# Features in 32x64 tiles from compact transposed probabilities, and a saturating addition for q's clip

## The chip, the cores and the metric

The kernel runs on one core of a Trainium2 chip. The metric is device time in microseconds, as the median of several runs. Five engines work side by side, each through its own program: TensorE (PE; its weight loads are listed as PEld), VectorE (DVE), ScalarE (ACT), GpSimd (POOL) and SyncE (SP), which only starts transfers here. They wait for each other by semaphores. The kernel is written in Bass: each engine's order is the order in which its program is written out, and no scheduler moves anything.

## The reference

```python
def attn(x, Wq, bq, Wk, bk, Wv, bv, Wo, bo):      # after the GRU, x is [128 (b), 32 (t), 256]
    q, k, v = x @ Wq + bq, x @ Wk + bk, x @ Wv + bv
    ...                                            # reshape to 4 heads of 64, over 32 positions
    weights = softmax(einsum('bdsh,bdth->bdst', q, k) / sqrt(d))
    feats = einsum('bdst,bdth->bdsh', weights, v)
    return feats.reshape(B, S, F) @ Wo + bo
def derivative(q, p, drive, coupling, bias):
    dq = q - q ** 3 / 3.0 - p + drive + tanh(q) @ coupling.T + bias
    dp = EPSILON * (q + ALPHA - BETA * p)
    return dq, dp
def rk4_step(q, p, drive, coupling, bias):
    ...                                            # four derivatives, at 0, DT/2, DT/2, DT
    q_next = clip(q + DT / 6.0 * (dq1 + 2 * dq2 + 2 * dq3 + dq4), -CLAMP, CLAMP)
    p_next = clip(p + DT / 6.0 * (dp1 + 2 * dp2 + 2 * dp3 + dp4), -CLAMP, CLAMP)
    return q_next, p_next
def ffn(x, w_gate, w_up, w_down):                  # bitlinear: 8-bit rows, ternary weights
    return bitlinear(silu(bitlinear(x, w_gate)) * bitlinear(x, w_up), w_down)
x = x + attn(gru(cond_2048, x, ...), ...)
x = x + ffn(rk4(cond_2048, cond_2048, x, ...), ...)
```

## The kernel before

The kernel works in three stages.

**The GRU**, 32 steps, up to 209 us. TensorE holds it; q and k of the attention are made beside it. Nothing of it is changed.

**Attention**, 209 to 294.5 us, in 8 rounds of 16 batch rows (4 groups `g` of 128 columns, each with 4 rows of 32 positions, `quads` j). In round i TensorE runs scores(i) (L374, 64 calls on tiles of 64 rows and 32 columns), values(i, 0) (L396, 12 matmuls), in three rounds a weight sum (L416), project(i-2, 0) (L436, 6 matmuls of 512 columns), values(i, 1), project(i-2, 1) and feats_of(i-1) (L410, 16 calls). An fp32 call of scores or feats appears as two matmuls and two weight loads. VectorE runs the softmax of the round (L934 maximum, L938 subtraction, L942 sum, L944 reciprocal, L946 product into `Pn`), then `turn(i)` (L955): four transposes of 32x512, one for each quad, put the 32x32 blocks of P on the diagonal of a 128x128 block of `PT`, whose other places are zero (GpSimd's two memsets L1243 at the stage's start, `s_zero`). So feats_of multiplies four batch rows at once with K = 128, three quarters of it zeros. Then `keep_feats` (L961) makes the low half of the features that `project` reads, once ScalarE has made the high half (L693), and `residual` (L967) adds the projection to x. ScalarE copies scores and values out of PSUM (L685, L678) and takes the exponential (L726).

**The RK4 and FFN stage**, 294.5 to 601.7 us, 32 steps t of four slots each. A slot starts with a seed that VectorE writes into PSUM (seed_1 L1042, seed_2 L1046, seed_3, seed_4), ScalarE makes tanh in two halves m (L756) and the scaled square (L759), TensorE adds the coupling and identity products to the seed (L461), VectorE makes w = cubic (L1066) and with L1072 the next point from PSUM and w. The last slot's L1072 writes to another part of PSUM (columns 128 to 256), and the clip L1161 makes q of the next step from it. GpSimd keeps the chain of p: v1 (L1273), uz (L1276), u3 (L1277), t1 (L1282), W3 (L1290), WZ (L1299), dq, and p of the next step (L1304); VectorE continues t1 to t2 (L1110), t3 and t4 (L1154). In the same step the FFN of earlier steps runs in a pipeline: `product` (L1085) multiplies the up projection (L560, four matmuls of 416 columns) with silu(gate), in two halves; the first half of step t-2 stands on VectorE right behind seed_1 of step t. ScalarE turns the product to integers (L775), TensorE transposes them (L497), ScalarE copies (L781).

Semaphores that matter: `s_next` counts L1072 (8 per step), `s_q` the clips (2 per step), `s_seed` the seeds (8 per step), `s_up` the up projections.

## Time and profile before

| | us |
|---|---|
| median of 3 runs | 604.24 (603.88 to 604.67) |
| the profiled execution, its own time | 603.75 |
| its span, first to last instruction | 601.7 |
| GRU, attention, last stage | 209.0, 85.5, 307.2 |
| busy: TensorE, VectorE, ScalarE, GpSimd | 572.9, 513.5, 390.1, 254.0 |
| mean granted TensorE clock | 0.997 |

Everything below is read from the one profiled execution. "issue" as the end of an idle time means that the engine waited for nothing that the profile shows. Busy times of matmuls are modelled, and neighbouring ones overlap a little.

### The profile page before, as it was taken

The page shows a single profiled execution, that of the slowest core. Times are in us where ns is not written, and L with a number is a line of the kernel's source. Part 1 is how long each engine was busy: PE and PEld are TensorE (multiplying, and loading weights), DVE is VectorE, ACT ScalarE, POOL GpSimd, SP SyncE. Part 2 cuts the span into 40 slices and gives each one's busy share as a digit, 9 for nine tenths or more (in the row PEclk, how much of TensorE's full clock was granted, in tenths as well). Part 3 has the DMA queues.
Part 4 walks back from the last instruction along what each step waited for, and adds up shares of the span by engine and source line. Part 5 has one row for each costly group of instructions (what it writes and reads, how often), then busy time and mean ns, then how long its engine had stood idle before and what let it go on. Part 6 is the DMA issues. An engine that isn't in the chain of part 4 may idle for free.

```text
span 601.7 us, 15742 instructions
## 1 busy us (share of the span) xinstructions
PE 572.9 (95%) x5692; PEld 521.0 (87%) x5692; DVE 513.5 (85%) x1547; ACT 390.1 (65%) x959; POOL 254.0 (42%) x401
## 2 busy tenths in 40 slices
PE   9999999999999988999978999999999999999997
PEld 8999999999999887888867788888888888888885
DVE  3777767776777768998999999999999999999996
ACT  3554454444544453464556888898898888888885
POOL 0423323233232264240155556556555555555550
PEclk9999999999999998999999999999999999999999
DMA  8500000000000000500000000000000000000001
GB/s 259 187 2 2 1 1 2 1 1 2 1 1 1 19 3 2 190 4 3 1 1 1 11 19 16 15 19 10 18 20 10 19 20 10 19 19 11 17 19 37
DMA packets 12523, 14.97 MB, mean 25 GB/s; under 512 B 1632, under 2 KB 10144, under 8 KB 12448
## 3 DMA queue, kind: packets, MB, share of 16 engines
q1 hardware_dynamic: 12448, 13.97, 7.0%
q8 instruction: 47, 0.77, 0.5%
q14 instruction: 28, 0.23, 0.1%
HBM read 9.78 MB, written 4.19 MB: 23 GB/s over the span
## 4 chain that ended last, share of the span: by engine, by line
PE 73%; DVE 13%; ACT 11%; issue 3%; DVEq 0%; POOL 0%; ACTq 0%; POOLq 0%
PE PS L461 23%; PE PS L313 17%; PE PS L336 13%; ACT q_s L775 5%; PE PS L436 4%; PE PS L513 4%; PE PS L534 3%; PE PS L497 3%; ACT k_s L756 2%; DVE big L955 2%; PE PS L396 2%; PE PS L319 2%; DVE PS L1072 1%; ACT PS L759 1%; DVE h_s L1161 1%
## 5 line engine op out<-in xcount | busy, mean ns | idle before, releaser
L461 PE MATMUL PS<-k_s,h_s 128*128 128x128 f32 x1024 | 160.6, 284 | 4.2 <-DVE PS L1046 2.0
L461 PEld LDWEIGHTS PS<-k_s,h_s 128*128 128x128 f32 x1024 | 131.7, 191 | 21.1 <-DVE PS L1060 9.8
L313 PE MATMUL PS<-part 128*128 128x256 f32 x900 | 115.6, 286 | 0.0
L313 PEld LDWEIGHTS PS<-part 128*128 128x128 f32 x900 | 109.8, 191 | 0.0
L756 ACT ACTIVATE k_s<-h_s 128x128 f32<-128x128 f32 x256 | 69.1, 306 | 49.8 <-DVE h_s L1161 29.0
L336 PE MATMUL PS<-big,wrk 128*128 128x128 f32 x744 | 88.4, 275 | 1.7 <-DVE big L913 1.7
L336 PEld LDWEIGHTS PS<-big,wrk 128*128 128x128 f32 x744 | 85.8, 192 | 2.3 <-DVE big L913 2.3
L1229 POOL COPY h_s<-big 128x256 f32<-128x256 f32 x32 | 21.5, 671 | 128.9 <-DVE big L913 128.9
L461 PE MATMUL PS<-h_s 128*128 128x128 f32 x384 | 74.3, 275 | 0.0
L461 PEld LDWEIGHTS PS<-h_s 128*128 128x128 f32 x384 | 58.3, 192 | 0.0
L650 ACT ACTIVATE big<-big 128x256 f32<-128x256 f32 x32 | 13.3, 416 | 63.2 <-DVE big L895 63.2
L1066 DVE SCALAR_TENSOR_TENSOR h_s<-PS,h_s 128x256 f32<-128x256 f32 x128 | 52.7, 412 | 0.3 <-ACT PS L759 0.2
L1072 DVE SCALAR_TENSOR_TENSOR h_s<-PS,h_s 128x128 f32<-128x128 f32 x192 | 50.1, 285 | 2.2 <-PE PS L461 0.8
L759 ACT ACTIVATE PS<-h_s 128x256 f32<-128x256 f32 x128 | 47.2, 369 | 1.4 <-DVE part L961 1.4
L640 ACT ACTIVATE big<-PS,bg 128x256 f32<-128x256 f32 x96 | 41.2, 467 | 6.8 <-DVE bg L852 5.8
L1085 DVE SCALAR_TENSOR_TENSOR q_s<-PS,q_s 128x416 f32<-128x416 f32 x64 | 41.0, 644 | 0.8 <-PE PS L560 0.8
L652 ACT ACTIVATE big<-big 128x256 f32<-128x256 f32 x32 | 13.4, 418 | 38.9 <-DVE big L903 38.9
L1304 POOL TENSOR_SCALAR h_s<-q_s 128x256 f32<-128x256 f32 x31 | 12.5, 402 | 59.0 <-DVE q_s L1154 59.0
L1290 POOL TENSOR_TENSOR h_s<-h_s,k_s 128x256 f32<-128x256 f32 x32 | 25.0, 780 | 29.1 <-DVE q_s L1110 27.9
L899 DVE SCALAR_TENSOR_TENSOR big<-PS,bh,big 128x128 f32<-128x128 f32 x64 | 19.5, 346 | 18.0 <-ACT big L650 18.0
L1299 POOL TENSOR_TENSOR q_s<-h_s,k_s 128x256 f32<-128x256 f32 x32 | 23.9, 748 | 23.2 <-DVE PS L1052 23.2
L775 ACT ACTIVATE q_s<-q_s,mag 128x832 f32<-128x832 f32 x29 | 30.9, 1067 | 0.0
(189 smaller groups left out, 1244.9 us busy)
## 6 DMA issues: line engine op xcount, KB each, us to landing
out<-q_s SPq DMA_DIRECT2D x32, 128.0 KB, 1.7
x_s<-in_xT SPq DMA_DIRECT2D x14, 256.0 KB, 6.1
k_s<-in_wgT SPq DMA_DIRECT2D x1, 832.0 KB, 5.3
k_s<-in_wuT SPq DMA_DIRECT2D x1, 832.0 KB, 7.2
k_s<-in_wih SPq DMA_DIRECT2D x3, 256.0 KB, 4.1
wrk<-in_whh SPq DMA_DIRECT2D x3, 256.0 KB, 4.3
h_s<-in_wdT SPq DMA_DIRECT2D x1, 768.0 KB, 7.5
x_s<-in_xT SPq DMA_DIRECT2D x4, 128.0 KB, 3.6
```

The source lines that it names most:

```text
L313: r = pe.matmul(p, y, x, start=i == 0, stop=i == len(passes) - 1)
L336: r = pe.matmul(PS[:, bank, m * 128:(m + 1) * 128], whh_s[:, k, (m0 + m) * 128:(m0 + m + 1) * 128], hprev[:, k, :], start=k == 0, stop=k == 1)
L436: r = pe.matmul(PS[:, bank, :], raw(w), raw(x), start=k == 0 and n == 0, stop=k == 1 and n == 2)
L461: return pe.matmul(PS[:, m, 0:128], w, x, start=False, stop=True, skip_group_check=True)
L640: ac.activation(gi[:, n % 2, m, :], bulk_bank(u), ACT.Identity, bias=bg[:, m:m + 1]).then_inc(s_gi, 1)
L756: ac.activation(cm(th[slot % 2], m), cm(src, m), ACT.Tanh).then_inc(s_th, 1)
L759: ac.activation(sqP, src, ACT.Square, scale=math.sqrt(cube[s])).then_inc(s_sq, 1)
L775: ac.activation(hf[:, 0:NI], hN[i % 2], ACT.Identity, scale=h_at(i, 4), bias=mag[:, 0:1]).then_inc(s_hf, 1)
L1066: ve.scalar_tensor_tensor(w_, sqP, cube[s] * own[s], src, ALU.subtract, ALU.mult).then_inc(s_w, 1)
L1072: ve.scalar_tensor_tensor(dst(m), PS[:, m, 0:128], of_ps[slot % 4], cm(w_, m), ALU.mult, ALU.subtract).then_inc(s_next, 1)
L1085: ve.scalar_tensor_tensor(hN[i % 2][:, at], pg[:, g], q_at(i, 3), sg[:, at], ALU.mult, ALU.mult).then_inc(s_hN, 1)
L1290: po_.tensor_tensor(two(W3), two(u3), I_at(t), ALU.add).then_inc(s_W3, 1)
```

## The change

Attention. The probabilities stay compact: `PT` is 128x512, and `turn` is one 128x512 transpose (the engine's transpose works in 32x32 blocks). feats_of makes 64 calls of K = 32, M = 64, N = 32 in 32x64 tiles in place of 16 of K = 128, M = 64, N = 128. The features stand in PSUM by quads (banks 4 to 7; in round 7 banks 1 and 2, in two halves with a wait between them), project reads them by a strided view, and the other banks move with them: values 4 to 2, project and the keep-warm matmuls 7 to 3. The memsets and `s_zero` go, values(0, 0) no longer waits for `s_qka`, and VectorE's keep_feats waits for both of ScalarE's halves.

Last stage. q and p are kept multiplied by lam = 3/c4, so that the last slot's new q is PS + w without a factor. A custom VectorE operation (`TENSOR_ADD_SAT`, addition with two limits) writes q in place of L1072 and L1161; the seeds, tanh and squares take the factor back in their scale. seed_1 waits for `s_q` and becomes a scalar_tensor_tensor. On GpSimd v1 stands behind the wait for seed_1, and t1 ahead of uz and u3.

```diff
-        PT = [big[:, 2048 + 2048 * r:4096 + 2048 * r].rearrange("p (u n) -> p u n", u=16) for r in range(2)]
+        PT = [big[:, 2048 + 512 * r:2560 + 512 * r] for r in range(2)]
...
-        feats = [PS[:, 5:7, :]] * 7 + [PS[:, 3:5, :]]
+        fb = lambda a, n: PS[:, a:a + n, :].rearrange("p b (h n) -> p (b h) n", h=2)
+        feats = [PS[:, 4:8, 0:256]] * 7 + [fb(1, 2)]
+        of_g = lambda a: a.rearrange("p (j g t) -> p g j t", j=4, g=4)
...
                 if (i, hf) == (0, 0):
                     pe.wait_ge(s_wv, 2)
                     pe.wait_ge(s_vs0, 1)
-                    pe.wait_ge(s_qka, 1)
...
                 pe.wait_ge(s_PT, i + 1)
-                for g in range(4):
-                    for hd in range(4):
-                        a = 64 * (hd % 2)
-                        r = pe.matmul(feats[i][a:a + 64, hd // 2, g * 128:(g + 1) * 128], Vs[i % 2][:, g, hd * 64:(hd + 1) * 64],
-                                      PT[i % 2][:, unit(g, hd), :], start=True, stop=True)
+                for js in ((0, 2), (1, 3)) if i == 7 else ((0, 1, 2, 3),):
+                    if js == (1, 3):
+                        r.then_inc(s_pv7, 1)
+                        pe.wait_ge(s_pv7, 1)
+                    for g in range(4):
+                        for kk in range(2):
+                            for j in js:
+                                for a in (0, 64):
+                                    hd = 2 * kk + a // 64
+                                    r = pe.matmul(feats[i][a:a + 64, j, (4 * kk + g) * T:(4 * kk + g + 1) * T],
+                                                  Vs[i % 2][quads[j], g, hd * 64:(hd + 1) * 64],
+                                                  PT[i % 2][quads[j], unit(g, hd) * T:(unit(g, hd) + 1) * T],
+                                                  start=True, stop=True)
                 r.then_inc(s_pv, 1)
...
             def turn(i):
-                if i < 2:
-                    ve.wait_ge(s_zero, i + 1)
-                else:
+                if i >= 2:
                     ve.wait_ge(s_pv, i - 1)
                 ve.wait_ge(s_P, i + 1)
-                for r in quads:
-                    o = ve.transpose(PT[i % 2][r, :, r], Pn[r, :, :])
-                o.then_inc(s_PT, 1)
+                ve.transpose(PT[i % 2], Pn.rearrange("p u n -> p (u n)")).then_inc(s_PT, 1)
...
                 for m in range(2):
                     if t:
-                        ve.wait_ge(s_next, 8 * t - 1 + m)
-                    ve.tensor_tensor(PS[:, m, 0:128], I_at(t)[:, m], cm(pn[t % 2], m), ALU.subtract).then_inc(s_seed, 1)
+                        ve.wait_ge(s_q, 2 * t - 1 + m)
+                    ve.scalar_tensor_tensor(PS[:, m, 0:128], cm(pn[t % 2], m), -1 / lam, I_at(t)[:, m], ALU.mult,
+                                            ALU.add).then_inc(s_seed, 1)
...
+            def last_next(t):
+                ve.wait_ge(s_w, 4 * t + 4)
+                for m in range(2):
+                    ve.wait_ge(s_ps, 8 * t + 7 + m)
+                    ve._custom_dve(bass.dve_ops.TENSOR_ADD_SAT, out=cm(qn[(t + 1) % 2], m), in0=PS[:, m, 0:128],
+                                   in1=cm(w_, m), s0=CLAMP * lam, s1=-CLAMP * lam).then_inc(s_q, 1)
...
-                nexts(4 * t + 3, lambda m: PS[:, m, 128:256])
-                for m in range(2):
-                    ve.wait_ge(s_next, 8 * t + 7 + m)
-                    ve.tensor_scalar(cm(qn[(t + 1) % 2], m), PS[:, m, 128:256], CLAMP, -CLAMP, ALU.min,
-                                     ALU.max).then_inc(s_q, 1)
+                last_next(t)
...
                     po_.wait_ge(s_q0, 1)
+                if t:
+                    po_.wait_ge(s_seed, 8 * t + 2)
                 if t < T - 1:
                     po_.tensor_scalar(v1, p, horner[0], 0.0, ALU.mult, ALU.add).then_inc(s_v1, 1)
-                if t:
-                    po_.wait_ge(s_seed, 8 * t + 2)
-                po_.tensor_scalar(uz, p, -n3, 0.0, ALU.mult, ALU.add).then_inc(s_uz, 1)
-                po_.tensor_scalar(u3, p, -n2, 0.0, ALU.mult, ALU.add).then_inc(s_u3, 1)
-                if t < T - 1:
-                    if t:
-                        po_.wait_ge(s_q, 2 * t)
                     po_.wait_ge(s_v1, t + 1)
                     po_.tensor_tensor(t1, v1, q, ALU.add).then_inc(s_t1, 1)
+                po_.tensor_scalar(uz, p, -n3 / lam, 0.0, ALU.mult, ALU.add).then_inc(s_uz, 1)
+                po_.tensor_scalar(u3, p, -n2 / lam, 0.0, ALU.mult, ALU.add).then_inc(s_u3, 1)
```

TensorE's order from values ahead of feats(0) to scores(3), before (`big` holds values and PT, `part` the split halves, `k_s,q_s` keys and queries):

```order
L396 MATMUL PS<-part 128x256 x24
L410 MATMUL PS<-big 64x128 x16
L374 MATMUL PS<-k_s,q_s 32x32 x64
L396 MATMUL PS<-part 128x256 x12
L436 MATMUL PS<-part 128x512 x6
L396 MATMUL PS<-part 128x256 x12
L436 MATMUL PS<-part 128x512 x6
L410 MATMUL PS<-big 64x128 x16
L374 MATMUL PS<-k_s,q_s 32x32 x64
```

and after:

```order
L400 MATMUL PS<-part 128x256 x24
L420 MATMUL PS<-big 64x32 x64
L379 MATMUL PS<-k_s,q_s 32x32 x64
L400 MATMUL PS<-part 128x256 x12
L448 MATMUL PS<-part 128x512 x6
L400 MATMUL PS<-part 128x256 x12
L448 MATMUL PS<-part 128x512 x6
L420 MATMUL PS<-big 64x32 x64
L379 MATMUL PS<-k_s,q_s 32x32 x64
```

The same places in the same order; L410's 16 calls have become L420's 64, directly ahead of the 64 of scores.

VectorE at the end of a step and the start of the next, before (`h_s` and `q_s` hold the step's buffers, `k_s` the drive and tanh):

```order
L1154 SCALAR_TENSOR_TENSOR q_s<-q_s,h_s 128x256
L1157 RECIPROCAL q_s<-q_s 128x1
L1072 SCALAR_TENSOR_TENSOR PS<-PS,h_s 128x128 x2
L1161 TENSOR_SCALAR h_s<-PS 128x128 x2
L1042 TENSOR_TENSOR PS<-k_s,h_s 128x128 x2
L1085 SCALAR_TENSOR_TENSOR q_s<-PS,q_s 128x416
L1066 SCALAR_TENSOR_TENSOR h_s<-PS,h_s 128x256
L1102 TENSOR_REDUCE q_s<-PS 128x1
```

and after:

```order
L1174 SCALAR_TENSOR_TENSOR q_s<-q_s,h_s 128x256
L1177 RECIPROCAL q_s<-q_s 128x1
L1092 ISA h_s<-PS,h_s 128x128 x2
L1054 SCALAR_TENSOR_TENSOR PS<-h_s,k_s 128x128 x2
L1105 SCALAR_TENSOR_TENSOR q_s<-PS,q_s 128x416
L1079 SCALAR_TENSOR_TENSOR h_s<-PS,h_s 128x256
L1122 TENSOR_REDUCE q_s<-PS 128x1
```

The two clips are gone, and the last slot's two L1072 are the two L1092; nothing else has moved.

GpSimd over the same turn, from p of the next step (L1304, after: L1315), before:

```order
L1304 TENSOR_SCALAR h_s<-q_s 128x256
L1273 TENSOR_SCALAR h_s<-h_s 128x256
L1276 TENSOR_SCALAR h_s<-h_s 128x256
L1277 TENSOR_SCALAR h_s<-h_s 128x256
L1282 TENSOR_TENSOR q_s<-h_s 128x256
L1290 TENSOR_TENSOR h_s<-h_s,k_s 128x256
```

and after:

```order
L1315 TENSOR_SCALAR h_s<-q_s 128x256
L1289 TENSOR_SCALAR h_s<-h_s 128x256
L1291 TENSOR_TENSOR q_s<-h_s 128x256
L1292 TENSOR_SCALAR h_s<-h_s 128x256
L1293 TENSOR_SCALAR h_s<-h_s 128x256
L1301 TENSOR_TENSOR h_s<-h_s,k_s 128x256
```

t1, the tensor_tensor into `q_s`, stands two places earlier.

## Rows read from the trace of the kernel before

**Rows 1.** Busy time by stage: stretch, length, PE, PEld, DVE, ACT, POOL, clock, DMA share.

```profile
209.00:294.50 85.50, 79.16 (x1600) 69.57 (x1600) 74.19 (x126) 43.98 (x68) 31.07 (x25) 0.98 0.11 36
294.50:601.70 307.20, 287.56 (x2365) 246.65 (x2363) 293.26 (x1067) 248.81 (x634) 160.68 (x278) 1.00 0.05 15
```

**Rows 2.** The page: the chain that ended last, by line.

```profile
PE PS L461 23%; PE PS L313 17%; PE PS L336 13%; ACT q_s L775 5%; PE PS L436 4%; PE PS L513 4%; PE PS L534 3%; PE PS L497 3%; ACT k_s L756 2%; DVE big L955 2%; PE PS L396 2%; PE PS L319 2%; DVE PS L1072 1%; ACT PS L759 1%; DVE h_s L1161 1%
```

**Rows 3.** TensorE's timeline, attention: start, us, engine, line, operation, [idle before it].

```profile
212.45 1.66 PE L396 MATMUL PS<-part 128*128 128x256 f32 x12 [0.21 <-ACT q_s L671]
...
217.68 1.03 PE L374 MATMUL PS<-k_s,q_s 64*32 64x32 f32 x97 [0.45 <-issue]
...
221.06 1.69 PE L396 MATMUL PS<-part 128*128 128x256 f32 x12 [0.69 <-ACT big L678]
222.91 1.97 PE L410 MATMUL PS<-big 128*64 128x128 f32 x32 [0.17 <-DVE big L955]
...
226.37 0.34 PE L374 MATMUL PS<-k_s,q_s 64*32 64x32 f32 x26 [0.48 <-issue]
226.64 1.70 PE L396 MATMUL PS<-part 128*128 128x256 f32 x12
230.63 2.78 PE L436 MATMUL PS<-part 128*128 128x512 f32 x6 [2.29 <-DVE part L961]
...
238.44 1.29 PE L374 MATMUL PS<-k_s,q_s 64*32 64x32 f32 x128
...
241.19 1.55 PE L436 MATMUL PS<-part 128*128 128x512 f32 x6
...
247.39 1.40 PE L374 MATMUL PS<-k_s,q_s 64*32 64x32 f32 x128
```

**Rows 4.** Stretches around project(0,0), TensorE alone; PEclk is the third number from the end.

```profile
230.50:232.00 1.50, 1.37 (x4) 0.59 0.00 0
232.00:234.00 2.00, 2.00 (x8) 0.50 0.03 8
```

**Rows 5.** VectorE's timeline, the first two turns.

```profile
219.92 2.85 DVE L955 STREAM_TRANSPOSE big<-big 32x512 f32<-32x512 f32 x4
...
226.85 2.85 DVE L955 STREAM_TRANSPOSE big<-big 32x512 f32<-32x512 f32 x4
```

**Rows 6.** The page, DMA queues: packets, MB, share of 16 engines.

```profile
q8 instruction: 47, 0.77, 0.5%
```

**Rows 7.** DMA traffic between 223.2 and 226.4, in 40 slices of 0.08 us.

```profile
DMA  0000000000700000000000000000000000000000
...
q8 instruction: 1, 0.02, 1.9%
```

**Rows 8.** TensorE's timeline, the last scores and values.

```profile
275.82 1.29 PE L374 MATMUL PS<-k_s,q_s 64*32 64x32 f32 x128
277.04 0.50 PE L396 MATMUL PS<-part 128*128 128x256 f32 x2
277.74 1.36 PE L396 MATMUL PS<-part 128*128 128x256 f32 x10 [0.20 <-issue]
```

**Rows 9.** All engines' timeline, the turn of one step into the next of the last stage.

```profile
488.11 0.87 PE L560 MATMUL PS<-h_s,q_s 128*128 128x416 bf16 x4
...
488.30 0.48 DVE L1161 TENSOR_SCALAR h_s<-PS 128x128 f32<-128x128 f32 x2
...
488.70 0.49 DVE L1042 TENSOR_TENSOR PS<-k_s,h_s 128x128 f32<-128x128 f32 x2
488.70 0.27 PEld L486 LDWEIGHTS PS<-ident,h_s 128*128 128x128 f32 x2
...
489.10 0.65 DVE L1085 SCALAR_TENSOR_TENSOR q_s<-PS,q_s 128x416 f32<-128x416 f32 x1
...
490.55 0.55 PE L497 MATMUL PS<-identh,q_s 128*128 128x128 f16 x7 [0.35 <-ACT q_s L775]
...
491.42 0.79 POOL L1290 TENSOR_TENSOR h_s<-h_s,k_s 128x256 f32<-128x256 f32 x1 [0.68 <-DVE q_s L1110]
```

**Rows 10.** VectorE's timeline, the first product of the last stage.

```profile
316.70 0.65 DVE L1085 SCALAR_TENSOR_TENSOR q_s<-PS,q_s 128x416 f32<-128x416 f32 x1 [0.80 <-PE PS L560]
```

More of the change, by code:

```diff
@@ L200, in build @@
         s_bulk, s_gi, s_qk, s_qka = sem("s_bulk"), sem("s_gi"), sem("s_qk"), sem("s_qka")
[L202 to L203 removed]
+        s_wv, s_vs0, s_wo, s_vhi, s_split = (
+            sem(n) for n in ("s_wv", "s_vs0", "s_wo", "s_vhi", "s_split"))
+        s_pv7 = sem("s_pv7")
         s_S, s_Vp, s_pv, s_o = sem("s_S"), sem("s_Vp"), sem("s_pv"), sem("s_o")
@@ L395, in values @@
                             pe.wait_ge(s_vs0, 2)
-                        r = pe.matmul(PS[:, 4, (g % 2) * 256:(g % 2) * 256 + 256], raw(x), raw(w), start=n == 0,
+                        r = pe.matmul(PS[:, 2, (g % 2) * 256:(g % 2) * 256 + 256], raw(x), raw(w), start=n == 0,
                                       stop=n == 5)
@@ L415, in weight_sum @@
                 pe.wait_ge(s_abs, w + 1)
-                pe.matmul(PS[:, 7, w:w + 1], ones[:, :], wsum[:, w:w + 1], start=True, stop=True).then_inc(s_wsum, 1)
+                pe.matmul(PS[:, 3, w:w + 1], ones[:, :], wsum[:, w:w + 1], start=True, stop=True).then_inc(s_wsum, 1)
             def project(i, m):
@@ L1241, in gpsimd @@
             po_.wait_ge(s_hb, T)
-            for r in range(2):
-                po_.memset(PT[r][:, :, :], 0.0).then_inc(s_zero, 1)
             for i in range(9):
```

80 lines of the change are left out of this document (42 added, 38 removed).

## The prediction

> **What bounds the kernel now.** The stages were read first. The GRU (0 to 209 us) is not touched by the change. Attention takes 85.5 us and TensorE is busy for 79.2 of them; the RK4/FFN stage takes 307.2 us, with VectorE busy for 293.3 and TensorE for 287.6 [rows 1]. The chain of work that ended last names L461 first, and counts the clip L1161 at only 1% [rows 2], so the last stage is a hand-over between TensorE, VectorE and ScalarE and not one engine's load.
>
> In attention I read TensorE's timeline, then what released it. From 238.44 to 247.39, scores(3) to scores(4), one round takes 8.95 us and nothing in it waits: TensorE is the bound there. The one long wait is 2.29 us ahead of the first project at 230.63, for VectorE's keep_feats [rows 3]. VectorE gets there late because each turn of P is four transposes, 2.85 us [rows 5]. After that idle stretch the granted clock is 0.59 and then 0.50 of full [rows 4], that is 1.2 GHz instead of 2.4, and the six matmuls of that project take 2.78 us where the same six take 1.55 later [rows 3].
>
> The same timeline shows something smaller that I take to decide this case. Twice a row of scores is cut by a gap put down to "issue": 0.45 us ahead of 217.68, with 97 of the 128 matmuls still to come, and 0.48 us ahead of 226.37, with 26 to come [rows 3]; a third gap, 0.20 us, stands at 277.74 [rows 8]. Each matmul has one weight load beside it (2365 and 2363 in the last stage, [rows 1]), so between the first two gaps lie 2 x (97 + 12 + 12 + 32 + 102) = 510 instructions, two times 255: the rest of scores(1), two halves of values, feats(0) and the head of scores(2). The page counts 47 instruction packets of 0.77 MB in all [rows 6], 16 KB each. One of them starts in the tenth of the 40 slices between 223.2 and 226.4, at 224.0; it takes 1.9% of 16 engines' 3.2 us, 0.97 us [rows 7], and TensorE goes on at 226.37. So TensorE's program seems to come in blocks of some 256, and a block cannot begin before its packet, asked for when the block before it began, has arrived. The lower bound from block start to block start: 2 x 102 = 204 instructions of scores(2) and 52 of the 64 of feats(0) ahead of the gap put the last start near 222.91 + 12 x 0.03 = 223.3, and it resumed at 226.37, so **3.1 us**. For the third gap, 252 instructions ahead of the two values matmuls, the start is that of scores(7), 275.82, and the resumption 277.74: **1.9 us** [rows 8].
>
> **The change, part by part.** Sums are against the profiled execution, 603.75 us; the median of before is 604.24, so 0.5 is added at the end.
>
> (a) Turn. One 128x512 transpose in place of four 32x512 ones. Four cost 2.85 us, one of 32x512 about 0.70; the elements per partition are the same, so I take 0.70 (lower end: 0.69 as an elementwise operation; upper end 2.85, if the 128 rows were worked off in fours). Saved 2.15 per block on VectorE. Two such turns precede keep_feats(0) [rows 5], 4.3 us, more than the wait of 2.29 [rows 3]: the wait goes, and next late is TensorE itself. With it the half clock goes: 2.78 - 1.55 = 1.2 us on the project and some 0.4 on the values behind it, together **-3.9**. In the later blocks TensorE does not wait for VectorE, and the saving there is worth nothing on the path.
>
> (b) Feats. 16 calls (32 matmuls, 1.97 us [rows 3]) become 64 calls, 128 matmuls and 128 weight loads, of a quarter of the columns. Each works in its own 32x64 tile, eight fit the array at once. The nearest row is scores, also 128 matmuls on eight tiles: 1.29 us. The other end is today's 1.97 or somewhat over, should the 64-column loads set the pace. I take 1.29, -0.68 for each of the six feats that stand in TensorE-bound rounds, **-4.1**.
>
> (c) Start. values(0,0) no longer waits for s_qka; project and feats banks change places; the GpSimd memsets go. 0.21 of wait at 212.45 and 0.17 ahead of feats(0) [rows 3]: **-0.4**. Today's issue gaps, 0.93 in all, are partly absorbed by the wait for L678 that follows: counted in (d).
>
> (d) Instruction blocks. In today's rounds feats (64) and scores (256) make 320 fast instructions. After, feats(i-1) and scores(i+1) stand back to back (TensorE's order in the section on the change), 512 fast ones in 2.6 us. Wherever the boundary falls, one whole block of 256 lies inside such a row, and takes 1.3 us where at least 1.9 to 3.1 are needed. That is a stall of 0.6 to 1.8 us in each of six rounds, and nothing covers it, since TensorE is the bound. The block behind the first row is short also, up to 1.0. Between 1.9 and 3.1 I take 2.9, since two of three gaps show 3.1: 6 x 1.6 + 1.0 = 10.6 us, against some 0.6 of today's gaps that this replaces: **+10.0**.
>
> The Trainium skill (Runtime: NRT & Kernel Launch, Instruction fetch mechanics) says that programs are refilled in blocks of 256 instructions and that crossing a boundary is "mostly hidden"; the block size agrees with the distance of the gaps here, the hiding not: 0.45 and 0.48 us are open. By its rule (d) would be near nothing, which is rival 1.
>
> (e) The clip. Two clips (0.48 the pair, 0.40 from the first to the seeds behind them) and the step through PSUM go; a saturating addition in place of L1072 writes q. The chain view suggests 0.2 from the clip and 0.2 from tanh, earlier by as much: 0.4 a step. But it buys only the time until the next thing that VectorE waits for: the product L1085 at 489.10, behind four L560 matmuls that begin at 488.11 and end at 488.98, and no later than these allow [rows 9]. In step 2 the same product visibly waits 0.80 for L560 [rows 10]. L560 stands on TensorE behind its own queue, which the clip doesn't move. From L1085 on VectorE runs without a gap to the next seed, and TensorE's pass L497 waits for ScalarE at the same time, 490.55. So the clip's 0.4 becomes wait ahead of L1085. I take 0.01 a step, 0.3 in all (0 to 0.08 x 31), and 0.4 for the first step, where no product stands: **-0.7**.
>
> (f) The saturating addition itself is not in the trace. Nearest: a two-input operation on 128x128 from PSUM or to it, 0.49 the pair (L1042), 0.20 apart. A custom one may be as fast, or slower by some tenths; up to 0.3 more a step disappears in the wait that (e) opens; beyond it each 0.1 costs 3 us. I take 0. Seeds change form at the same 0.29. Scales in tanh and square ride in the same instruction: 0.
>
> (g) GpSimd. v1 waits for the seeds now and t1 comes ahead of uz and u3. Same instructions, same wait ahead of W3 for VectorE's t2 (0.68 idle, [rows 9]); the held 0.41 fits into it: 0.
>
> **Sum.** -3.9 -4.1 -0.4 +10.0 -0.7 = +0.9: 604.65 for the profiled execution, 605.1 on the median. By the ends of block time alone: 1.9 gives 6 x 0.6 = 3.6 in (d), 598; 3.1 gives 606.3; if feats keep today's 1.97 with 3.1, (b) is nothing, a block in the row takes 1.3 to 2.0 and each stall is some 0.35 shorter, 608.3. As two of three gaps stand at the upper end, and (b) can only be worse than taken, I put the forecast a little above the sum, **605.6 us**.
>
> **Rivals.** 1. Blocks arrive ahead (faster). Then (d) is -0.6 to +3.6 and the kernel lands at 595 to 599. For it: the third gap's 1.9, and the last stage runs without such gaps; against it, 256 of its instructions take 16.6 us (4728 in 307.2, [rows 1]). By the skill's rule (above) this is the case. 0.25. 2. The hand-over pays (faster). The chain view is right, L560 comes early too, and each step is 0.3 to 0.4 shorter: -9 to -12 on top, 595. Against: L1085 starts right at the end of L560. 0.09. 3. The idle stretches of (d) bring back the half clock (slower). 2.29 us of idle did it once [rows 3, 4] and cost 1.6; stalls of 1.6 to 1.8 in each round could, 0.45 did not. From 1.6 us idle on it decides: three to six times 1.6 on 605, or feats at 1.97 and more: 609 to 613. 0.15. 4. The addition does not do what it is for (no change of its own, or slower by 0.1 to 0.2 beyond its cover): +3 to +6, 608 to 611. 0.06. The forecast's own case (602.5 to 608): 0.45.
>
> **How the numbers follow.** 0.2% (1.2 us) is about what a measurement of this kernel can tell from none: 603.0 to 605.4 is no change. The main case puts 0.04 under it, 0.17 within, 0.24 over. With rivals 1 and 2 faster has 0.37, with 3 and 4 slower 0.45, the rest 0.18. For 8 in 10 the range reaches from 596.5, inside rivals 1 and 2, to 611, inside rival 3.
>
> **What would show it.** In the changed profile: (a) L955 once per block at 0.7, no wait ahead of project(0,0), clock 1.0 to 294 us. (b) L420, 128 matmuls, 1.3 us when not cut. (d) in six rounds an "issue" idle of 1 to 2 us inside L420 or L379, at distances of 256 instructions. If these gaps are under 0.5, rival 1 holds; if the clock falls behind them, rival 3. (e) L1105 with an idle of 0.3 to 0.4 for TensorE's L560 successor in each step, and the last stage within 1 us of its 307.2; one shorter by 9 or more is rival 2. (f) L1092 at 0.28 to 0.30. The forecast is wrong most likely in the block time, which rests on three gaps.

## The result, and the profile after

The changed kernel takes **621.84 us** (median of 4 runs, 620.37 to 626.09), the kernel before 604.06 beside it. The ratio is 1.031, with a 95% interval of 1.029 to 1.034. It is slower, as forecast, but by 18 us where the forecast said 1.5, and outside the range of 596.5 to 611. The profiled execution took 621.29 us with a span of 619.3, 17.6 us more than before.

The page of the changed kernel: the instruction packets, and the chain that ended last by engine.

```profile
q8 instruction: 53, 0.87, 0.6%
...
PE 79%; DVE 12%; issue 6%; ACT 2%; DVEq 0%; POOL 0%; POOLq 0%
```

53 packets in place of 47 [rows 6], and "issue", time in which an engine waited for nothing that the profile shows, is now 6% of the chain (3% before). Busy time by stage (columns as in [rows 1]), over fixed stretches:

```profile
209.00:294.50 85.50, 69.65 (x2069) 61.99 (x2067) 48.93 (x78) 37.82 (x58) 24.83 (x15) 0.88 0.11 36
294.50:619.00 324.50, 300.79 (x2668) 259.06 (x2668) 296.62 (x1029) 258.68 (x645) 164.77 (x286) 0.99 0.04 15
```

Between 209 and 294.5 us, where TensorE was busy for 79.2 us [rows 1], it is busy for 69.7 now at a mean clock of 0.88, and attention isn't over. Its last projects start at 304.14 and the keep-warm matmuls behind them at 311.29; before, the keep-warm matmuls started at 294.39. So 16.9 us of the 17.6 are there by the start of the last stage. Of these 0.7 lie ahead of attention: every step of the GRU comes 0.73 later from the first on, since the opening matmuls are slower in this execution (the first 24 of L318 take 5.90 us for 5.35). TensorE's timeline in attention (start, us, engine, line, operation, idle before it) answers to [rows 3]:

```profile
223.34 1.49 PE L420 MATMUL PS<-big 32*64 32x32 f32 x128
...
225.90 1.24 PE L379 MATMUL PS<-k_s,q_s 64*32 64x32 f32 x122 [0.88 <-issue]
...
229.46 0.99 PE L400 MATMUL PS<-part 128*128 128x256 f32 x7 [1.53 <-issue]
230.28 1.57 PE L448 MATMUL PS<-part 128*128 128x512 f32 x6
...
238.97 0.45 PE L379 MATMUL PS<-k_s,q_s 64*32 64x32 f32 x32 [1.90 <-issue]
...
253.32 1.00 PE L379 MATMUL PS<-k_s,q_s 64*32 64x32 f32 x70 [4.59 <-issue]
254.25 2.93 PE L400 MATMUL PS<-part 128*128 128x256 f32 x12
256.98 2.73 PE L448 MATMUL PS<-part 128*128 128x512 f32 x6
...
277.50 0.43 PE L379 MATMUL PS<-k_s,q_s 64*32 64x32 f32 x21 [2.00 <-issue]
...
302.15 2.06 PE L420 MATMUL PS<-big 32*64 32x32 f32 x102 [1.34 <-issue]
304.14 7.32 PE L448 MATMUL PS<-part 128*128 128x512 f32 x24
```

The long wait for L961 ahead of the first project (230.63 in [rows 3]) is gone, and feats takes 1.49 instead of 1.97. But ten gaps with the releaser "issue" add up to 15.4 us: 0.46, 0.88, 1.53, 1.90, 4.59, 0.45, 0.51, 2.00, 1.73 and 1.34. Matmuls and weight loads counted together in the trace, with the few records of TensorE's sequencer between them, each of these gaps stands 256 or 512 instructions behind the one before, to within one. And what follows five of the six gaps over 1.3 us (not the 1.53) is slow: twelve values matmuls take 2.93 us where 1.69 is usual, six project matmuls 2.73 where 1.57 is, the last 24 7.32. The windows show the clock there (stretch, length, PE busy, PEclk, DMA share, GB/s):

```profile
249.00:253.30 4.30, 0.00 (x0) 0.93 1.04 397
253.30:259.50 6.20, 6.18 (x88) 0.50 0.18 56
...
304.00:311.30 7.30, 7.30 (x36) 0.77 0.01 2
```

Behind the gap of 4.59 us TensorE runs at 0.50 of the full clock, the level of 1.2 GHz, for 6 us, and the last projects have 0.77 on the mean. And in that gap the transfers run at 397 GB/s: the FFN's weights.

The last stage, the turn of a step, answers to [rows 9]; behind it the one line of who held up L1105:

```profile
505.45 0.29 DVE L1092 CUSTOM_DVE_ANT_0 h_s<-PS,h_s 128x128 f32<-128x128 f32 x1 [0.17 <-PE PS L473]
505.47 0.87 PE L572 MATMUL PS<-h_s,q_s 128*128 128x416 bf16 x4
505.66 0.49 DVE L1054 SCALAR_TENSOR_TENSOR PS<-h_s,k_s 128x128 f32<-128x128 f32 x2
...
506.31 0.41 POOL L1289 TENSOR_SCALAR h_s<-h_s 128x256 f32<-128x256 f32 x1 [0.80 <-DVE PS L1054]
...
506.45 0.65 DVE L1105 SCALAR_TENSOR_TENSOR q_s<-PS,q_s 128x416 f32<-128x416 f32 x1 [0.30 <-PE PS L572]
...
507.86 0.41 POOL L1293 TENSOR_SCALAR h_s<-h_s 128x256 f32<-128x256 f32 x1
...
508.08 0.34 DVE L1059 SCALAR_TENSOR_TENSOR PS<-h_s,k_s 128x128 f32<-128x128 f32 x1
```

```profile
  PE PS L572: 9.9, 30
```

The addition L1092 takes 0.29, seed_1 follows at once, and VectorE then idles for 0.30 until the up projection is done: 9.9 us in 30 steps. Steps are 9.12 us apart in place of 9.08.

### The profile page after: what moved, and what is told of

Its sections match the earlier page's. It is cut to its first block, busy times and chain, and to the rows that moved or that the text cites. A ratio compares the mean times of both kernels' runs of the same rounds, so it can differ in the third digit from the quotient of the medians.

```text
span 619.3 us, 17184 instructions
## 1 busy us (share of the span) xinstructions
PE 576.7 (93%) x6460; PEld 526.0 (85%) x6460; DVE 490.8 (79%) x1459; ACT 393.5 (64%) x959; POOL 251.5 (41%) x399
## 4 chain that ended last, share of the span: by engine, by line
PE 79%; DVE 12%; issue 6%; ACT 2%; DVEq 0%; POOL 0%; POOLq 0%
PE PS L473 23%; PE PS L318 17%; PE PS L341 12%; PE PS L400 5%; PE PS L448 4%; PE PS L572 4%; PE PS L525 4%; PE PS L546 3%; DVE q_s L1105 3%; DVE h_s L1085 2%; DVE q_s L1122 2%; PE PS L420 2%; PE PS L379 2%; PE PS L324 2%; DVE PS L1059 1%
## 5 line engine op out<-in xcount | busy, mean ns | idle before, releaser
L318 PE MATMUL PS<-part 128*128 128x256 f32 x900 | 115.6, 286 | 0.0
L318 PEld LDWEIGHTS PS<-part 128*128 128x128 f32 x900 | 109.8, 191 | 0.0
L769 ACT ACTIVATE k_s<-h_s 128x128 f32<-128x128 f32 x256 | 72.3, 307 | 47.2 <-DVE h_s L1085 29.4
L1085 DVE SCALAR_TENSOR_TENSOR h_s<-PS,h_s 128x128 f32<-128x128 f32 x192 | 50.1, 285 | 2.1 <-PE PS L473 0.8
L1105 DVE SCALAR_TENSOR_TENSOR q_s<-PS,q_s 128x416 f32<-128x416 f32 x64 | 41.0, 643 | 9.9 <-PE PS L572 9.9
L1315 POOL TENSOR_SCALAR h_s<-q_s 128x256 f32<-128x256 f32 x31 | 12.5, 402 | 59.0 <-DVE q_s L1174 59.0
L400 PE MATMUL PS<-part 128*128 128x256 f32 x192 | 31.5, 320 | 2.3 <-issue 1.5
```

The lines of the kernel that those rows point to most:

```text
L318: r = pe.matmul(p, y, x, start=i == 0, stop=i == len(passes) - 1)
L400: r = pe.matmul(PS[:, 2, (g % 2) * 256:(g % 2) * 256 + 256], raw(x), raw(w), start=n == 0, stop=n == 5)
L769: ac.activation(cm(th[slot % 2], m), cm(src, m), ACT.Tanh, scale=(-1 if s == 3 else 1) / lam).then_inc(s_th, 1)
L1085: ve.scalar_tensor_tensor(dst(m), PS[:, m, 0:128], of_ps[slot % 4], cm(w_, m), ALU.mult, ALU.add if slot % 4 == 2 else ALU.subtract).then_ ...
L1105: ve.scalar_tensor_tensor(hN[i % 2][:, at], pg[:, g], q_at(i, 3), sg[:, at], ALU.mult, ALU.mult).then_inc(s_hN, 1)
```

## The experiments

Theory: TensorE's program arrives in blocks of 256 instructions, at a limited rate; feats and scores back to back use them up faster, and the clock falls by half behind the idle time. In the last stage, the clips' time has turned into a wait for the up projection. Runs in which one part is done alone, undone or mended follow, and a direct measurement.

### Each half of the change alone

att_only is the attention part on the last stage of before, last_only the other way round.

> The attention part of the change on the last stage of before. Theory (program blocks arrive late where feats and scores stand back to back, and the idle time halves the clock): the whole loss is here. The attention stage is longer than the kernel before's by 15 to 17 us, 'issue' gaps of 0.5 to 4.6 us inside L420/L379, and the last stage keeps its 9.08 us period: 619 to 622 us. Rival (the loss is half in the last stage, from the custom addition and the moved GpSimd order): 611 or less.

> The last-stage part alone (scaling, saturating addition, GpSimd order), attention as in before. Theory: the clip's time becomes a wait for the up projection (L572 in the changed kernel), and the period goes from 9.08 to 9.13 us as in the changed kernel: 604.5 to 605.5 us. Rival (the last stage gains once attention no longer disturbs it): a period of 8.7 to 9.0 us, 592 to 602 us.

Measured: att_only 622.98 us (618.37 to 624.96, ratio 1.031, 1.026 to 1.036); last_only 604.16 (603.52 to 605.78), ratio 1.0014, 0.9998 to 1.003. The whole loss is in attention. The steps of att_only's last stage are the 9.08 us of before, those of last_only 9.12. On the whole time the last-stage part is worth nothing, either way.

### Is it the number of instructions?

padded is the kernel before, with small calls on constants behind feats(0) to feats(5):

```diff
                 r.then_inc(s_pv, 1)
+                if i < 6:
+                    for n in range(48):
+                        j, c = n // 2 % 2, 64 * (n % 2)
+                        at = 32 * (n // 4)
+                        pe.matmul(PS[c:c + 64, 2 + j, at:at + 32], ones[32 * j:32 * j + 32, 0:64],
+                                  ones[32 * j:32 * j + 32, 0:32], start=True, stop=True)
```

> The kernel before, whole, with 48 extra small matmul calls (96 matmuls and 96 weight loads on constants, into unused banks) right behind each of feats(0) to feats(5), so that 256 instructions of feats and padding stand ahead of the 256 of scores as in the changed kernel; turn, banks and last stage are those of before. Theory (the number of instructions back to back makes the gaps): 'issue' gaps of 1 to 2 us in most of the six rounds, one of 3 to 5 near 250 us where the weights are loaded, half clock behind those over 1.5: 3 to 5 us for the padding itself and 12 to 20 for the gaps, 618 to 628 us. Rival (the strided reads, the 32-row tiles or the new banks of the changed feats make them): 607 to 610 us, gaps as in before.

Measured: 625.22 us (623.64 to 626.03), ratio 1.036, 1.033 to 1.038. The gaps come at the same instructions as in the changed kernel (ahead of the last 32, 70, 21 and 61 matmuls of a row of scores), each by 0.3 to 0.5 us shorter. TensorE's timeline of padded:

```profile
241.60 0.36 PE L374 MATMUL PS<-k_s,q_s 64*32 64x32 f32 x32 [1.62 <-issue]
...
257.55 1.00 PE L374 MATMUL PS<-k_s,q_s 64*32 64x32 f32 x70 [4.16 <-issue]
...
283.60 0.33 PE L374 MATMUL PS<-k_s,q_s 64*32 64x32 f32 x21 [1.49 <-issue]
...
297.20 0.79 PE L374 MATMUL PS<-k_s,q_s 64*32 64x32 f32 x61 [1.34 <-issue]
```

The transpose, the strided reads and the banks of the changed feats are not in this kernel, so they do not make the gaps. What it shares with the changed kernel is the number of instructions, and also the 32x64 tiles of the padding calls; that such tiles stand without gaps when slow instructions lie between them is shown by feats_mixed below. The padding took 1.6 us a round, twice what I had expected. Up to the keep-warm matmuls padded is 21.8 us behind the kernel before: some 9 us are the padding's own work, 9.9 the gaps (11.0 less 1.1 of before), and half clock adds some 5 us more than before, against the wait of 2.29 us, which is gone.

### Fast instructions apart

feats_apart issues feats_of(i-1) between values(i,0) and project(i-2,0), feats_mixed between project(i-2,0) and values(i,1). The edit of feats_mixed:

```diff
-                if i == 8:
-                    feats_of(7)
...
                     project(i - 2, 0)
+                if 1 <= i < 9:
+                    feats_of(i - 1)
                 if i < 8:
                     values(i, 1)
...
-                if 1 <= i < 8:
-                    feats_of(i - 1)
```

> The changed kernel with feats_of(i-1) issued between values(i,0) and project(i-2,0), so that 24 values and 12 project instructions stand between each 256 of scores and each 256 of feats; the same instructions and the same work. Theory: every block of 256 now holds at least 36 slow instructions and lasts some 4 us, longer than the 3.1 to 3.3 us from block to block: no 'issue' gap over 0.5 us from the third round on, clock 1.0, attention 8 to 9 us shorter than in before, 596 to 598 us. Rival 1 (small tiles themselves slow the supply of instructions, wherever they stand): gaps stay, 615 to 620. Rival 2 (gaps come whenever a block is under 5 us, since packets queue behind the weight loads): one gap of 2 to 4 us at 250 us stays, 600.

Measured: 613.38 us (612.0 to 613.78), ratio 1.016, 1.013 to 1.018. That is 8.5 less than the changed kernel, not the 24 that I expected. Its timeline:

```profile
233.92 0.31 PE L420 MATMUL PS<-big 32*64 32x32 f32 x7 [1.76 <-issue]
...
242.84 0.69 PE L420 MATMUL PS<-big 32*64 32x32 f32 x45 [0.27 <-issue]
...
254.52 1.06 PE L420 MATMUL PS<-big 32*64 32x32 f32 x83 [3.01 <-issue]
...
294.51 8.66 PE L448 MATMUL PS<-part 128*128 128x512 f32 x24 [0.69 <-DVE x_s L977]
```

My sum was wrong for the side with values only. A block that spans scores, the 24 instructions of values and feats takes 1.69 + 1.1 to 1.2, not 4 us, and so three gaps of 0.2 to 0.3 stay in the later rounds, one of 1.76 ahead of 233.92 and 3.01 at the weight loads. The gap of 1.76 was not followed by half clock: from 231 to 240 us the clock was 1.00. The end is also slow: 24 projects in 8.66 us, at a mean clock of 0.65.

> The changed kernel, with feats_of(i-1) between project(i-2,0) and values(i,1): 36 slow instructions on either side of each 256 fast ones from the third round on, the same instructions in all. Theory: a block of 256 takes at least 3.2 + 1.1 = 4.3 us, more than 3.3, so no 'issue' gap from scores(3) on but the one near 250 us (2 to 3 us, behind the weight loads); the first three rounds keep theirs: 605 to 609 us. Rival (the supply is slower than 4.3 us per 256 once it has to catch up): gaps in every round, over 612.

Measured: 611.11 us (610.09 to 613.08), ratio 1.012, 1.009 to 1.015, above the 605 to 609 that I expected. Its timeline:

```profile
236.62 1.29 PE L379 MATMUL PS<-k_s,q_s 64*32 64x32 f32 x128
...
245.31 1.29 PE L379 MATMUL PS<-k_s,q_s 64*32 64x32 f32 x128
...
251.81 1.11 PE L420 MATMUL PS<-big 32*64 32x32 f32 x90 [1.60 <-issue]
...
289.90 2.58 PE L448 MATMUL PS<-part 128*128 128x512 f32 x6 [3.46 <-DVE x_s L977]
292.41 3.95 PE L420 MATMUL PS<-big 32*64 32x32 f32 x128
296.29 6.41 PE L448 MATMUL PS<-part 128*128 128x512 f32 x18
```

From 234 to 286 us the rounds now run without a gap but for 1.60 behind the weights and one of 0.75. (Three waits of 0.25 for the weight sums are there as before.) scores(4) follows scores(3) by 8.69 us where 8.95 stood before [rows 3]: 0.26 us is what the small tiles give a round when the program keeps up, under half of the 0.68 of my term (b). That the time is still 611 lies mostly in the end: project(6,0) waits 3.46 us for residual(5,0), which VectorE does last, feats(7) takes 3.95 at 0.50 of the clock, and the 18 projects behind it 6.41, part of them at half clock (0.66 on the mean).

### The weight loads

loads_apart is the changed kernel with the four loads issued at four places, mixed_loads_pool adds that and GpSimd's old order to feats_mixed:

```diff
-            sp.wait_ge(s_Vp, 8)
-            sp.dma_start(coup, kp(coupT)).then_inc(ld_coup, 16)
             for i, w in enumerate((wgT, wuT)):
+                sp.wait_ge(s_Vp, 8 + i)
                 sp.dma_start(halves(w_src[i]), kp(w)).then_inc(ld_w[i], 16)
+            sp.wait_ge(s_Vp, 11)
```

> The changed kernel, with the 2.8 MB of weights that are issued together after values(3,1) issued one by one: w_gate then, w_up after values(4,0), w_down after values(5,0), coupling after values(6,0). Theory (the packet of the program waits behind these loads): the gap of 4.59 us falls to 1.7 to 2.5, and no new one over 2.5 appears: 2 to 3 us less than the changed kernel, 618 to 620. Rival (that gap has another cause): it stays at 4 to 5 us, 621 to 622.

Measured: 618.88 us (618.16 to 621.32), ratio 1.026, 1.023 to 1.029. The time is in the range of the theory; the gap of 4.59 is 2.71 here, a little over the 2.5 that I had as its bound, and the one ahead of it 2.06:

```profile
240.33 0.47 PE L381 MATMUL PS<-k_s,q_s 64*32 64x32 f32 x32 [2.06 <-issue]
...
252.59 0.81 PE L381 MATMUL PS<-k_s,q_s 64*32 64x32 f32 x70 [2.71 <-issue]
```

> The last two edits together, and GpSimd's old order. Theory: the three effects add up: no gap over 0.5 us from scores(3) on, clock 1.0 there, period of a step 9.08 us: 599 to 603 us. Rival (the load of weights moves into blocks that were not short of time before, or the late weights hold up ScalarE): 604 to 608.

Measured: 610.4 us (609.54 to 612.65), which is feats_mixed again. The rival holds in what it says of the gap; its 604 to 608 left out the slow end, which this kernel shares with feats_mixed. The gap at 251.81 is gone, and a new one stands just behind the third load, w_down, which is issued at 257.69:

```profile
264.61 0.42 PE L422 MATMUL PS<-big 32*64 32x32 f32 x2 [3.51 <-issue]
```

By the count of instructions the block before the gap started at 259.07, right behind that load, and its packet of the program started only at 261.97, 2.9 us later. The loads of w_gate and w_up, issued at 244.46 and 248.72, delayed the next packets too (they started 2.1 and 1.8 us behind their blocks' starts), but those blocks took 4.2 to 4.4 us to work off, and no gap of note came. So not every load of 0.8 MB costs a gap; spacing alone moved this one.

### The end, and loads in a chain

mixed_tail is feats_mixed with feats_of(7) ahead of project(6,0) again, and residual(5,0) earlier on VectorE:

```diff
-                if 2 <= i < 7:
+                if i >= 2:
                     residual(i - 2, 0)
                 if i == 7:
                     weight_top(0, 0)
...
-            residual(5, 0)
             residual(5, 1)
```

> The changed kernel with feats_of(0 to 6) between project and values(i,1) as in the run feats_mixed, feats_of(7) back ahead of project(6,0), and residual(5,0) ahead of normal(7) on VectorE. Theory: the idle 3.46 us ahead of project(6,0) and the half clock behind it (L448 x18 in 6.41 us, L420 in 3.95) fall away, the rest is as in feats_mixed: 602 to 605 us. Rival (project(6,0) waits for keep_feats(6) anyway and the clock halves as in feats_apart): 607 to 610.

Measured: 607.0 us (604.69 to 607.24), ratio 1.006, 1.004 to 1.008; its profiled execution took 604.69. The wait of 3.46 us is gone and the clock is 1.00 in the last 10 us of attention. The median lies at the edge of the rival, the profiled execution in the range of the theory. The first three rounds still carry 4.1 us of gaps (0.80, 0.86, 0.86, 1.53), the weights 1.49. That is what this feats costs with the order mended: it is no gain yet.

mixed_tail_chained_split issues each piece of the weights when the last has landed (w_down follows in the same way in three pieces, and the coupling weights come last instead of first):

```diff
             for i, w in enumerate((wgT, wuT)):
-                sp.dma_start(halves(w_src[i]), kp(w)).then_inc(ld_w[i], 16)
+                for k in range(2):
+                    sp.dma_start(halves(w_src[i])[:, k], kp(w)[:, k]).then_inc(ld_w[i], 16)
+                    sp.wait_ge(ld_w[i], 16 * k + 16)
```

and signals the up projection by halves (next section).

> The run mixed_tail, with the FFN weights loaded in seven pieces of 0.26 to 0.43 MB, each issued when the one before has landed, and the up projection split. Theory: the 1.6 us gap near 250 us and the half clock behind it shrink (a packet of the program waits for one piece, 1 us), -2 to -3 us, and the last stage gives 6 to 9: 592 to 597 us. Rival (the chain of pieces comes too late for ScalarE's weight_abs, or the last stage does not pay): 600 to 604.

Measured: **595.39 us** (594.04 to 598.79), ratio 0.987, 0.985 to 0.990. That is in the range of the theory. Beside 0.59, 0.60, 0.85 and 0.22 in the first rounds its remaining gaps in attention are:

```profile
229.27 0.99 PE L404 MATMUL PS<-part 128*128 128x256 f32 x7 [1.53 <-issue]
...
261.02 0.30 PE L424 MATMUL PS<-big 32*64 32x32 f32 x2 [0.77 <-issue]
```

No gap stands near 250 us any more: there the packets start 1.0 to 1.2 us behind the start of their blocks, where it was 3.7 in the changed kernel. The mean clock of the profiled execution is 1.0. Two edits meet in this run, but they act in different stages. The keep-warm matmuls start at 291.0 us (294.4 in before, 294.6 in mixed_tail), and from there to the end it takes 301.0 us (307.3 and 308.1). So of the gain on before some 3.4 us are attention and 6.2 the last stage. Chained loads were not tried on the kernel before, which had no gap at its loads.

### What the clips were worth

Both kernels get the same edit, the one before and the last-stage part of the change: the up projection is signalled after two of its four matmuls, and the product's first half waits for these alone.

```diff
                     for g in range(2):
                         for k in range(2):
                             r = pe.matmul(pg[:, g], qiT[:, k, :], wu_q[:, k, g * 416:(g + 1) * 416],
                                           start=k == 0, stop=k == 1)
-                    r.then_inc(s_up, 1)
+                        r.then_inc(s_up, 1)
...
-                    ve.wait_ge(s_up, i + 1)
+                    ve.wait_ge(s_up, 2 * i + 1)
                     product(i, 0)
```

> The kernel before, with the up projection L560 signalled after each half, so that the product's first half (L1085) waits for two of its four matmuls, 0.4 us earlier. Theory (in before the product starts when the clips and the seeds ahead of it on VectorE are done, which is the same moment as the end of L560): 0 to 0.1 us per step at most, 601.5 to 604.5 us. Rival (L560 alone sets the product in before): 0.3 to 0.4 per step, 592 to 595 us.

> The last-stage part of the change alone, with the same split of the up projection. Theory (the clips' 0.4 us has become a wait for the up projection, 0.30 us per step in the changed kernel): with the product's first half waiting for half of it the wait goes, and the period falls from 9.13 to 8.8 to 8.9 us: 595 to 598 us. Rival (TensorE or ScalarE sets the period as soon as VectorE has slack): 9.05 or more, 602 to 604.

Measured: before_up_split 602.14 us (601.8 to 603.49), ratio 0.998, 0.997 to 0.999, with steps of 9.07; last_up_split **598.17** (596.64 to 599.05), ratio 0.991, 0.989 to 0.993, with steps of mostly 8.89. VectorE in last_up_split, and below it GpSimd in the same stretch:

```profile
502.53 0.29 DVE L1083 CUSTOM_DVE_ANT_0 h_s<-PS,h_s 128x128 f32<-128x128 f32 x1 [0.17 <-PE PS L463]
502.74 0.49 DVE L1045 SCALAR_TENSOR_TENSOR PS<-h_s,k_s 128x128 f32<-128x128 f32 x2
503.18 0.65 DVE L1096 SCALAR_TENSOR_TENSOR q_s<-PS,q_s 128x416 f32<-128x416 f32 x1
...
505.04 0.61 DVE L1121 SCALAR_TENSOR_TENSOR q_s<-q_s,h_s 128x256 f32<-128x256 f32 x1
```

```profile
503.88 0.73 POOL L1285 TENSOR_TENSOR q_s<-h_s 128x256 f32<-128x256 f32 x1
...
504.94 0.44 POOL L1287 TENSOR_SCALAR h_s<-h_s 128x256 f32<-128x256 f32 x1
```

The idle 0.30 ahead of the product is gone, and the product starts 0.65 us after the second addition instead of 1.00. Without the addition the same edit leaves the steps at 9.07. Of the 1.8 us by which its median is lower, 0.4 are in the last stage of the profiled execution. Most of the rest goes with a short stretch of half clock, which 3 of its 12 measurements show (a mean clock of 0.997 for 1.000) and 11 of the 17 of the kernel before. Without the edit the addition brings nothing. Together they bring 0.18 a step. That is less than the 0.3 that I had from the wait, and the last rows show one reason: t2 (the row of 0.61) takes 0.20 more than its usual 0.41. I had put that down to t1 coming late from GpSimd, but t1 (L1285) is done at 504.61, 0.43 us before t2 starts. What runs beside t2 is the scaling L1287, from 504.94 on, as in the next section.

### GpSimd's held product

pool_undone is the changed kernel with v1 ahead of the wait for seed_1, and uz, u3, t1 in the old order.

> The changed kernel with GpSimd's old order: v1 ahead of the wait for seed_1, then uz, u3, t1. Theory P (the 0.05 us by which the period of a step is longer comes from GpSimd's two scalings now running beside VectorE's seed_2, L1059, 0.34 us instead of 0.29): period back to 9.08 us, 1.4 us less than the changed kernel, L1059 at 0.29. Rival (it comes from the custom addition or from the seeds' new wait): period stays 9.13, same time as the changed kernel within 0.5 us. Attention is not touched and stays at its lengths.

Measured: 618.92 us (617.44 to 620.2), steps of 9.08. The period is back, L1059 is at 0.297 on the mean in place of 0.312, and the whole is 2.9 less than the changed kernel, where I had expected 1.4; of these 1.3 are the steps (0.045 x 28), and the rest lies ahead of the last stage, where the edit changes nothing of the program. What the held product avoids, and what it costs, can both be read. In pool_undone, GpSimd and VectorE:

```profile
502.19 0.41 POOL L1287 TENSOR_SCALAR h_s<-h_s 128x256 f32<-128x256 f32 x1
502.25 0.69 DVE L1054 SCALAR_TENSOR_TENSOR PS<-h_s,k_s 128x128 f32<-128x128 f32 x2
```

v1 beside seed_1 makes the pair take 0.69 instead of 0.49. Since the product waits for L572 anyway, that costs nothing. In the changed kernel (above) v1 stands behind, and now GpSimd's scaling at 507.86 lies beside seed_2 (508.08, 0.34 instead of 0.29), where nothing hides it.

In these runs it went with where VectorE reads. The operations that grew, seed_1, seed_2 and t2, have both inputs in SBUF. Others with the same scalings beside them, whose one input is in PSUM, did not grow: in the kernel before the product L1085 (489.10, with L1276 from 489.27 on beside it) takes 0.65, and the cubic L1066 behind it (489.67, beside L1277) 0.41. And it went with the order: the scaling had begun first each time, and VectorE's operation grew by what the scaling still had to run less some 0.14 us (on the median 0.34 left and 0.20 more for seed_1 and t2, 0.19 left and 0.05 more for seed_2 in the changed kernel, 0.17 left and 0.03 more for seed_2 in last_up_split). Where GpSimd began second, as W3 does behind seed_2 in before, seed_2 kept its 0.29, and W3 took 0.78 where the other tensor_tensors take 0.73. The two remaining runs ask whether this turns once the product no longer waits:

> The run last_up_split with GpSimd's old order (v1 ahead of the wait for seed_1). Theory 1 (without the wait for L572 nothing hides the 0.2 us by which v1 beside seed_1 lengthens it, 0.69 for the pair in place of 0.49): period 8.95 to 9.05 us, 1.5 to 4 us slower than last_up_split. Theory 2 (the held v1 makes t1 late, and VectorE's t2 takes 0.61 us for it in last_up_split instead of 0.41, so that the old order gives 0.2 back): the two cancel, within 1 us of it.

> The fastest version so far with GpSimd's old order. Theory 1: 1.5 to 4 us slower, 597 to 599; theory 2: the same, 595 to 596.

Measured: 596.71 us (596.38 to 598.14), ratio 0.990, 0.988 to 0.993, steps of 8.87, against 8.89 of last_up_split; and **594.29 us** (593.52 to 595.13), ratio 0.985, 0.983 to 0.987, the fastest of all versions here. The two orders differ by 0.02 a step in favour of the old one. Theory 1 is out. Theory 2 has the size right and the reason wrong: the old order gives t2 its 0.41 back since no scaling runs beside it, and pays about as much at seed_1 (0.68 for the pair in last_up_split_pool, with v1 beside it).

### The interval itself

probe puts 640 small calls, ten blocks of instructions, between attention and the last stage of the kernel before, where nothing else is transferred.

> The kernel before with 640 small matmul calls on constants (1280 matmuls and 1280 weight loads, ten blocks of 256 instructions) between attention and the last stage, where no other transfer runs. Theory: TensorE works a block off in about 1.3 us (1.5 at the pace of L420 in the changed kernel) and waits for the next, block start to block start 3.3 us throughout: nine gaps of 1.8 to 2.0 us, 33 us in all, and half clock from the first long gap on. Rival (the first blocks are there already, the later ones come slower): some blocks without a gap, then gaps over 2.5 us.

Measured, in a single execution: 638.98 us. TensorE's timeline, the windows (columns as above) and what the DMA engines moved in 40 slices of 0.9 us:

```profile
299.94 2.60 PE L480 MATMUL PS<-ones 32*64 32x32 f32 x128 [1.03 <-issue]
303.67 26.40 PE L480 MATMUL PS<-ones 32*64 32x32 f32 x914 [1.12 <-issue]
```

```profile
299.94:301.00 1.06, 1.06 (x72) 1.00 0.08 15
301.00:302.60 1.60, 1.54 (x70) 0.57 0.00 0
302.60:303.70 1.10, 0.04 (x4) 0.50 0.00 0
```

```profile
GB/s 0 0 0 18 0 0 0 18 0 0 0 18 0 0 0 18 0 0 0 18 0 0 0 0 18 0 0 0 18 0 0 0 18 0 0 0 18 0 0 0
```

There are two gaps, 1.03 and 1.12 us. Only the two intervals that end in them tell what the supply allows: by the count of instructions 3.1 and 3.7 us from block start to block start. Behind them packets still come some 3.6 us apart, but there the clock is 0.50 (from 305 to 330 us throughout), 128 pairs take some 3.7 us of work (914 in 26.40), and the engine itself sets the pace. Neither theory nor rival had this: I expected nine gaps, and half clock made the work of a block so long that only two came. Half clock came here without any long gap: it is at 0.57 on the mean from 301.0 to 302.6, behind the gap of 1.03 and ahead of that of 1.12. Whether the gap or the small matmuls themselves did it, the probe cannot tell apart. Together with the 1.76 us in feats_apart, which were not followed by half clock, it shows that the length of the gap alone does not decide, and that the point "from 1.6 us on" of my third rival is no threshold.

## Why the prediction was wrong

- **Direction and mechanism, right.** The program's blocks decide, in attention, where the forecast put them, and rival 1 (they arrive ahead) is out. The Trainium skill (Runtime: NRT & Kernel Launch, Instruction fetch mechanics) says that crossing a block is "mostly hidden"; in this stage it is not, 15.4 us are open.
- **(d), mis-sized: the first step that failed.** The term was 10.6 us and measured 14.9 without the first gap, which before had too: 12.1 in the six rounds for 9.6, 1.5 behind the first row for 1.0, and 1.3 that was not counted. The six rounds did not stall alike, by 1.6 each, but by 0.45 to 4.59. The block interval was taken from three gaps as if it were a constant of 2.9. In the traces it has two parts. From the start of a packet to the start of the block that had waited for it, it is nearly constant: 2.2 to 2.7 us at every gap of before and after. From the start of the block ahead to that of the packet it is 0.3 to 1.1 at most of them, once 2.5, and 3.7 in the stretch with the 2.8 MB of weights, which makes an interval of 6.2 (block at 247.17, packet at 250.84, next block at 253.32). The third gap of before, whose 1.9 us I took as the lower end, fits: its packet started 0.3 us ahead of the block, 2.2 ahead of the resumption. The trace of before had the load in the same place, but no block ran short there, so no gap showed it. The uncounted 1.34 us stand in the row feats(6), feats(7) at the end.
- **The half clock, put at nothing in the sum: the second step that failed.** Rival 3 should have been in the sum, not beside it. It came five times, at 1.0 to 2.5 us each, near its price of 1.6: by the rows, 1.2 + 0.2 behind 238.97, 1.2 + 1.2 behind 253.32, 1.2 + 0.1 + 1.0 behind 277.50, 1.0 behind 290.59, 0.9 + 1.6 at the end, 9.6 us, where before had 1.6. I had it as an alternative with 0.15, though by my own numbers most stalls would be 1.6 and the one known stretch with half clock followed 2.29. Its price started from a sum with (d) too small: the two errors add up, and so even its 609 to 613 fell short (three to six times 1.6 on 605 is 609.8 to 614.6, and not 613). The range shared this: the sum of 605.1 had no half clock at all in it, and the 9.6 alone pass 611; with the 4.3 more of (d) it is 619.0. The last stage (+1.4), the opening of the GRU (+0.7), the 1.1 unassigned below and -0.4 in the other terms lead to 621.8.
- **(a), (b), (c), nearly right.** The turn is one operation of 0.70 per block; the wait ahead of project(0,0) went, though 1.53 of "issue" took its place. Feats takes 1.49, not 1.29, but gave 0.48 in all eight blocks: -3.8 for -4.1 on TensorE (feats_mixed shows only 0.26 a round of it in the period).
- The balance of attention: +14.3 gaps (15.4 less 1.13 of before), +8.0 clock, -3.8 feats, -3.4 waits (2.29, 0.71, 0.21, 0.17) make +15.1 of 16.2; 1.1 stays unassigned.
- **(e), right.** The clips' time became the wait of 0.30 ahead of L1105, the period did not fall, and the pair of split runs shows that this wait, not TensorE's own load, held the gain. The first two steps, where no product stands, gave 1.1, where I had 0.4 for the first.
- **(f), right:** 0.27 to 0.29, like L1072.
- **(g), wrong by sign.** "0" was for the wait ahead of W3, which did stay. What I did not look at is who runs beside whom: moved by 0.5 us, the scalings lie beside seed_2 and lengthen each step by 0.05, +1.3 in all. With the 1.1 of (e), and some 0.4 more from the last seed_1 to the end, the last stage gave +0.7 instead of -0.7.

## What to carry to other kernels

Count instructions, not only time: where a rewrite puts several hundred short ones in a row on one engine, its program must arrive as fast as it runs, and a smaller tile that halves the work can make it slower. Keep slow instructions between the fast rows, and issue large loads in pieces that wait for one another where such a row stands. And before costing a saving on one engine, look for the wait right behind it: the saturating addition paid nothing until the product no longer waited for all of the up projection.

## What the runs showed of the hardware

- A block of 256 TensorE instructions (16 KB) took 3.1 and 3.7 us from start to start with nothing else transferred (probe, the two intervals that end in a gap), 1.9 to 3.6 at most gaps of before and after, once 5.2, and 6.2 beside 397 GB/s of loads. From the start of a packet to the start of the block that had waited for it, it was 2.2 to 2.7 us in before and after, also beside the loads; beside these the packet started late (3.7 us behind the block ahead). With short loads in a chain, each waiting for the one before, it started 1.0 to 1.2 us behind (mixed_tail_chained_split).
- A gap of 1.03 us between blocks of small matmuls was followed by 0.50 of the clock, which stayed there for the 26 us of such matmuls behind (probe). Gaps of 0.45 and 0.48 in before, and of 1.53 in after and 1.76 in feats_apart, were not. In feats_apart the clock also fell around feats(7), with its small tiles and two waits of 0.43 and 0.69.
- Small matmuls on 32x64 tiles with 32 columns took 1.49 us for 128, scores on 64x32 tiles 1.29.
- A one-input scaling on GpSimd beside a scalar_tensor_tensor of VectorE with both inputs in SBUF lengthened the latter by 0.03 to 0.2 us (seed_2 0.32 and t2 0.61 in last_up_split, the pair of seed_1 0.69 in pool_undone). The scaling had begun first, and the growth was what it still had to run less some 0.14 us. Those with an input in PSUM took 0.65 and 0.41 beside it in before, as elsewhere. A tensor_tensor of GpSimd that began behind seed_2 left that at 0.29 and took 0.78 itself, for 0.73.
